# Two buffers for the weighted expert rows, and GpSimd's scatter of a step issued behind its second addition of states

## The reference, cut to what matters

```
# mamba, for each of 8 batches, d = 256 channels, 16 states
x_ssm, gate = split(xn @ in_w + b);  x_conv = silu(conv4(x_ssm));  B, C = x_conv @ bc_w;  dt = softplus(x_conv @ dt_w)
for t in range(512): h = h * exp(dt[t] * A) + dt[t] * B[t] * x_conv[t];  y[t] = sum_n h[:, n] * C[t, n] + x_conv[t] * D
layernorm((y * silu(gate)) @ out_w + xn)
# mixture of experts, 8 experts, two of them for each of 4096 tokens
xn + sum_over_chosen_experts( weight * (silu(xn @ w1[e] + b1[e]) @ w2[e] + b2[e]) )
```

## Time and profile before

| | us |
|---|---|
| median of 3 runs (lowest, highest) | 936.59 (936.52, 938.7) |
| the profiled execution, its own time | 936.73 |
| its span, first to last instruction | 934.3 |
| busy: PE, DVE, ACT, POOL | 787.8, 787.8, 664.3, 601.2 |
| ScalarE's `weigh` waiting for a scatter to land, 16 times | 22.0 |
| GpSimd's scatter waiting for `weigh`, 40 times | 107.6 |

### The profile page before, as it was taken

The page is one execution under the profiler, slowest core; times in us unless marked ns, Lnnn a source line. Parts: engine busy times, 40 slices in busy tenths (PEclk is TensorE's granted clock), DMA queues, the critical chain, the costliest instruction groups (busy, mean ns, idle before and its releaser), DMA issues.

```text
span 934.3 us, 14382 instructions
## 1 busy us (share of the span) xinstructions
PE 787.8 (84%) x4533; PEld 634.1 (68%) x4533; DVE 787.8 (84%) x774; ACT 664.3 (71%) x1134; POOL 601.2 (64%) x384
## 2 busy tenths in 40 slices
PE   3993669978998899888989899889989997899852
PEld 2662647857776677677876777677768786778741
DVE  6818839798889968998899698989899889989993
ACT  1433668777688768876886878886878788869930
POOL 3571515757477757876767756884787487758861
PEclk9996989999999999999999999999999999999985
DMA  9939437568566865797668775786577667877731
GB/s 298 389 142 345 173 109 242 138 205 272 180 209 199 255 222 187 209 278 217 212 203 241 238 239 152 233 273 203 185 219 256 215 210 222 244 226 228 227 90 22
DMA packets 81927, 201.00 MB, mean 215 GB/s; under 512 B 7936, under 2 KB 41216, under 8 KB 81728
## 3 DMA queue, kind: packets, MB, share of 16 engines
q1 hardware_dynamic: 61424, 171.46, 53.4%
q0 software_dynamic: 19168, 26.59, 14.9%
q10 hardware_dynamic: 1264, 2.05, 0.7%
HBM read 174.38 MB, written 26.61 MB: 215 GB/s over the span
## 4 chain that ended last, share of the span: by engine, by line
DVE 36%; PE 27%; ACT 10%; issue 9%; DMA 6%; SPq 1%; POOL 1%; DVEq 0%; ACTq 0%; POOLq 0%
DVE ps_drive L935 13%; PE ps_up L1229 11%; DVE ring L942 9%; DVE ps_drive L928 7%; PE ps_yx L1243 6%; DMA bc_scratch<-sp 6%; PE ps_fr L1160 5%; ACT L787 3%; DVE xx L909 2%; ACT da L760 2%; PE ps_fr L1185 1%; PE ps_up L1223 1%; SPq L524 1%; DMA out<-yo,sid 1%; PE ps_up L1288 1%
## 5 line engine op out<-in xcount | busy, mean ns | idle before, releaser
L592 POOL TENSOR_TENSOR y<-y,ring 128x1024 f32<-128x1024 f32 x126 | 325.5, 2583 | 59.1 <-ACT y L751 51.8
L935 DVE TENSOR_TENSOR_SCAN ps_drive<-da,ps_drive 128x1024 f32<-128x1024 f32 x128 | 293.7, 2295 | 41.5 <-ACT da L760 37.8
L1229 PEld LDWEIGHTS ps_up<-xgt,w1s 128*128 128x128 f32 x2272 | 284.7, 197 | 17.9 <-issue 9.6
L1229 PE MATMUL ps_up<-xgt,w1s 128*128 128x128 f32 x2272 | 284.6, 280 | 0.0
L1243 PE MATMUL ps_yx<-w,ht 128*128 x1136 | 270.7, 382 | 0.0
L1243 PEld LDWEIGHTS ps_yx<-w,ht 128*128 128x128 f32 x1136 | 206.4, 192 | 28.8 <-issue 5.0
L581 POOL DMA_INDIRECT out<-yo,sid x71 | 117.9, 1660 | 147.0 <-ACT yo L802 107.6
L787 ACT ACT_TABLE_LOAD x143 | 183.5, 1283 | 2.5
L760 ACT ACTIVATE da<-gd,col 128x511 f32<-128x511 f32 x256 | 168.3, 710 | 0.0
L928 DVE TENSOR_TENSOR ps_drive<-ps_u,rep 128x1024 f32<-128x1024 f32 x128 | 157.4, 1229 | 9.5 <-DVE ring L942 0.5
L942 DVE TENSOR_TENSOR ring<-ps_drive,rep 128x1024 f32<-128x1024 f32 x128 | 156.5, 1223 | 3.9
(11 more groups left out here) (161 smaller groups left out, 724.1 us busy)
## 6 DMA issues: line engine op xcount, KB each, us to landing
w1s<-in_we SPq DMA_DIRECT2D x71, 1024.0 KB, 7.3
rep<-bc_scratch SPq DMA_DIRECT2D x128, 512.0 KB, 4.4
w<-in_we SPq DMA_DIRECT2D x8, 1024.0 KB, 11.9
w<-in_x SPq DMA_DIRECT2D x8, 512.0 KB, 11.0
xn_scratch<-da SPq DMA_DIRECT2D x8, 512.0 KB, 7.2
out<-w POOLq DMA_DIRECT2D x8, 512.0 KB, 6.2
xnt_scratch<-xx SPq DMA_DIRECT2D x8, 512.0 KB, 5.7
xx<-xnt_scratch SPq DMA_DIRECT2D x8, 512.0 KB, 3.3
```

The source lines that it names most:

```text
L592: pool.tensor_tensor(y[:, :, :], y[:, :, :], ring[:, g % RING, :, :], ALU.add).then_inc(s_sum, 1)
L935: dve.tensor_tensor_scan(states, da[:, g % DECAYS, :, :].rearrange("p k l -> p (k l)"), states, 0.0, ALU.mult, ALU.add).then_inc(s_scanned, 1)
L1229: mm = pe.matmul(bank[:, c * P:(c + 1) * P], w1s[:, q, k, at:at + P], xgt[:, k, :], start=False, stop=(c == 3 and k == KD - 1))
```

## The change

`yo` gets two buffers. `weigh(j)` writes buffer `j % 2` and waits for scatter j-2 instead of scatter j-1. On GpSimd the scatter of a step moves from between the two additions to behind the second one (and so behind `add_eps` in step 2 and `newton` in step 3; it stays ahead of `gated` in step 7 and of `finish` and `add_out` in step 4).

```diff
-        yo = sb("yo", [P, D])
+        yo = sb("yo", [P, 2, D])
...
-                    pool.indirect_dma_start(out[:, :], bass.IndirectOffsetOnAxis(ap=sid[:, s:s + 1], axis=0), yo[:, :], None,
+                    pool.indirect_dma_start(out[:, :], bass.IndirectOffsetOnAxis(ap=sid[:, s:s + 1], axis=0), yo[:, s % 2, :], None,
...
                     if i < IN and not (last and i == IN - 1):
                         add_state(b, i, 0)
-                    if not (last and i == STEPS - 1):
-                        scatter(s, b, i)
                     if i == 2 and prev is not None:
                         add_eps(prev)
                     if i == 3 and prev is not None:
                         newton(prev)
                     if i < IN and not (last and i == IN - 1):
                         add_state(b, i, 1)
+                    if not (last and i == STEPS - 1):
+                        scatter(s, b, i)
                     if i == IN - 1 and not last:
                         gated(b)
...
-                    if positive(j):
-                        act.wait_ge(s_scattered, j * 16)
-                    act.activation(yo[:, :], yx_y, ACT.Copy, scale=wslot[:, bass.ds(j, 1)]).then_inc(s_weighed, 1)
+                    if j > 1:
+                        act.wait_ge(s_scattered, (j - 1) * 16)
+                    act.activation(yo[:, j % 2, :], yx_y, ACT.Copy, scale=wslot[:, bass.ds(j, 1)]).then_inc(s_weighed, 1)
```

## The result

The changed kernel takes 972.68 us (median of 6 runs, 970.68 to 976.56), the kernel before 937.64 us beside it (6 runs, 932.55 to 939.34): a ratio of 1.037, 95% interval 1.0344 to 1.0397. Forecast were 955.0 us and a range of 940 to 963. The direction was right, but the time lies above the range, and half of the loss was not foreseen. The profiled execution took 971.84 us, with a span of 969.7 us; TensorE's granted clock fell on average from 0.961 to 0.938. Where the times of one kernel fall into two groups over 1.5% apart, the lower group is the one to compare.

What follows compares the result with a forecast made beforehand. Bound taken: a recurring round of about 98 us through VectorE's scans and taps, the B and C store, ScalarE and TensorE. Terms +29.4, -2.6, -7.8, -0.7 gave +18.3 on 936.73: 955 us, range 940 to 963.

Steps and rivals of the forecast that it cites:

- pairs of taps: VectorE's taps 2 and 3, steps 2 and 3 of seven batches: 14 pairs delayed 2.1 us each, +29.4 us.
- tap 1 of step 2: VectorE's tap no longer blocked by GpSimd's first addition, which ends sooner: about 1.12 us in seven batches, -7.8 us.
- the pair already paid: Step 3 of the first batch: its early scatter already made the pair of taps take 4.15 us, so -2.6 us.
- What comes: GpSimd's second addition, released by the second `times_c`, gets between taps 2 and 3: 2.1 us a pair, bounds 0 to 2.63.
- The rule of the Trainium skill: Two-input VectorE and SBUF-reading GpSimd instructions exclude each other entirely; by it alone 2.4 us a pair, total 959.
- What goes: Step 2: first addition ends at 366.5, before tap 1 at 367.43, giving back 1.12 us in seven batches, -7.8 us.
- Step 3: `newton` between additions ends before the second `times_c`, so full price, margin 0.8 us; rival that it shields: 942.4, 12 in 100.
- The two buffers: Of 16 `weigh` waits for scatters removed, one of 0.71 us stands in the chain: -0.7 us, bounds 0 and -22.0.
- Behind the taps: Step 4: `add_out` and GpSimd's queue behind it some 3 us late, users far, L917 covered: no cost counted.
- L917's cover: dt operation L917: another addition ahead costs 2.36 us, inside the scan's 3.90 us wait; nothing, or 2 us a batch uncovered.
- The rival whose number came closest, 962.8: Tap 1 of step 2 stays blocked, 955.0 + 7.8 us; shares 13 in 100 with L917's cover breaking.
- the other half of that rival: L917's cover breaks, counted as 7 x 1 us: 962; shares 13 in 100 with tap 1 staying blocked.

Runs made afterwards that it cites:

- order away: `add_out` of batches 0 to 6 sent to unread scratch rows, no scatter waits either way: kernel before 0.9955, changed 1.0178, scatter 4 between additions 1.0177, scatters 2-4 between 0.9882.
- the changed kernel without the order: Changed kernel with `add_out` of batches 0 to 6 sent to unread scratch rows, waiting for no scatter and holding none: 951.83 us, 1.0178.

## Why the prediction was half right

The loss in four parts, from the ratios (1.000 is 936.6 us here; each ratio is good to some 0.002, so each part to about 3 us, and the last, which has three of them, to about 4):

| part | from | measured us | forecast us |
|---|---|---|---|
| pairs of taps | 1.0177 - 0.9882 | +27.6 | +29.4 |
| tap 1 of step 2, the pair already paid, `weigh` | 0.9882 - 0.9955 | -6.8 | -11.1 |
| step 4's scatter late, order away | 1.0178 - 1.0177 | 0 | 0 |
| the order, after less before | (1.0370 - 1.0178) - (1.0000 - 0.9955) | +13.8 | 0 |
| sum | | +34.6 | +18.3 |

That is the loss along one path, with the taps priced where the order is away. With the order in place the same pairs are worth 19 to 31 us, depending on where the scatter of step 4 stands, so a part's number holds for this path and not for each part by itself.

**What comes** was right: a waiting addition gets between two operations that are queued back to back, in 14 pairs of 14, at 1.98 us each where I had 2.1. The runs with taps moved or scatters put back both show it; 14 x 1.98 is 27.7. The rule of the Trainium skill that I set beside it ("SBUF — State Buffer", Who interferes with whom) agrees with the trace; the addition that meets tap 2 lasts 2.73 us for 2.36, and tap 3 waits for it. The 2.4 us for a pair were too much, as an addition adds 1.98.

**What goes** was right in place (1.85 to 0.75 us, seven times) and came to about 4 us less in sum, which is hardly more than the uncertainty. Part of it is visible: in the kernels with scatters 2 and 3 between, which this row is measured by, tap 1 of step 3 takes 0.92 to 1.07 us in six of seven batches, where it took 0.72.

**Step 3**: `newton` did not shield the pair; all pairs of step 3 took 3.5 us. The margin was about the forecast 0.8 us: in the shown batch `newton` ends at 391.56 and tap 2, which starts at 391.68, would be over at 392.4. **The two buffers**: -0.7 forecast, 0.9998 measured with buffers alone.

**Behind the taps** is the step that failed. It had the size of the first delay right: `add_out` some 3 us late even against the late batch (it goes out at 414.12, 37.8 us behind tap 1 at 376.28, where it was 32.2; of these 5.7 us the taps make 2 x 1.98 - 1.1 = 2.9, and 2.8 are its own). Then it said: "Their users are far: the gathered rows are needed a step later, and VectorE may run four states ahead", and took nothing for it. The runs put it at 14 us more than before, 18 in all. Three things were wrong.
- I followed the users of the moved scatter's neighbours, and not the landing. The scatter of step 5 waits for `add_out`, which waits for the scatter of step 4. In that batch it leaves 48.8 us behind tap 1 (425.07), where it was 40.3: the 2.8 us have become 5.6. In that batch the chain of the kernel before already ran through a scatter's landing (7.34 us from 417.89, up to the `weigh` at 425.31), so there was no slack to count on. I had noted both waits in the description of the kernel and priced only `add_out`'s.
- I took its landing time as given. The transfer that landed in 6.8 us takes 10.1 in its new place, and the kernel with step 4's scatter put back has 7.6. What goes with it is the next load of expert weights (1 MB). Over the 18 traces and batches 1 to 6 of each, 48 `add_out` transfers have such a load issued between 1.3 us before and 2.2 us after them, and land in 9.9 to 13.3 us; the 55 whose next load is 3 us and more away land in 5.6 to 8.8. The store of B and C and a load of `rep` go out close to the weights, so which of the three slows it isn't isolated.
- "A step later" is not a whole step of slack. The gather that goes out at 303.24 before lands at 310.51, 7.3 us later and well over the median of 4.1, and is turned by TensorE at 311.83, which leaves 1.3. After, it goes out at 310.71 and lands at 320.87, and TensorE turns it at 320.91.

The fear that I did price in that part, L917's cover, was no cost: L917 got faster (the median before was 3610 ns). In the rows around it GpSimd's second addition, now ahead of the scatter, is over or nearly so when L917 starts. GpSimd's waits for landings are not needed for that: in the changed kernel without the order the median is 1216. With the order (shortest, median, longest in ns):

```profile
L917 DVE SCALAR_TENSOR_TENSOR gd<-xs,sp x8: 1216/1468/1828, 132.9 to 847.2; 128x1024 f32<-128x1024 f32 x8
```

The rival whose number came closest, 962.8, was right for none of its reasons. The price of the other half of that rival is also wrong as written: the text before it has 2 us a batch if the cover is gone, and the rival takes 7 x 1 us; with 2 it would have been 969, outside the range.

What stays open: how the 18 us of the order divide between the queue itself and the slower landing of `add_out` in it, and over gathers, `gated`, late additions and the slower clock behind the stalls. These run side by side, and closing one or two of them gave 0.001 to 0.005.

## What to carry to other kernels

When a transfer's issue is moved, follow its landing, not only the engine's queue: write down who waits for the landing, who waits for that one's landing, and compare the sum with the slack once more after the other terms of the change have used part of it. A chain of accumulating transfers on one output is like an engine of its own, with a time for each link, and that time is not fixed: it depends on what goes out beside the link. And a wait that GpSimd does ahead of an operation can be what keeps it off VectorE's two-input work: here the order with the scatters of steps 2, 3 and 4 left in place is the one that gains (0.9965), if little.

## What the runs showed of the hardware

- A waiting GpSimd addition is released by the `times_c` behind which the pair of taps is queued, and the outcome never varied: 3.50 to 3.52 us, in 14 of 14 pairs, in each of the kernels that have it. So these two engines also meet with no semaphore between them.
- Here TensorE works at half its clock for a while after a late gather, which lengthens the stall's cost. It waits 4.20 us for the rows (first line). Then 16 matmuls take 3.62 us and the next 16 take 1.96:

```profile
425.12 0.44 PE L1209 MATMUL ps_up<-ident,xg 128*128 128x128 f32 x2 [4.20 <-DMA xg<-xn_scratch,gid]
...
429.26 3.62 PE L1229 MATMUL ps_up<-xgt,w1s 128*128 128x128 f32 x16
...
433.10 1.96 PE L1229 MATMUL ps_up<-xgt,w1s 128*128 128x128 f32 x16
```

  The same stretches by windows (the number behind POOL's is the granted clock): 0.50, which is 1.2 GHz, and then 1.00, which is 2.4 GHz.

```profile
429.20:432.90 3.70, 3.70 (x18) 3.58 (x17) 3.56 (x3) 3.67 (x6) 3.58 (x2) 0.50 0.97 316
433.10:435.10 2.00, 2.00 (x19) 1.99 (x18) 1.97 (x3) 1.97 (x4) 1.38 (x1) 1.00 0.70 287
```

- A scatter of 128 rows of 1 KB with accumulation lands in a median of 6.4 us before and 5.4 after, and in up to 9.8 in the changed kernel, not much less than the 512 KB of `add_out` (6.8 before).
- The same 512 KB take 9.9 to 13.3 us to land when a weight load of 1 MB is issued within some 2 us of them, and 5.6 to 8.8 when it is 3 us and more away (103 transfers in 18 traces).
